# Five attention blocks of a decoder: the turned maxima are added to the queries in PSUM instead of on VectorE

## What is computed

```
Q = (x @ wq.T + bq).reshape(B, S, 16, 8)      K, V likewise (K, V from ctx in the cross blocks)
score  = einsum('bhqd,bhkd->bhqk', Q, K) / sqrt(8)
attn_w = softmax(score, axis=-1)
out    = einsum('bhqk,bhkd->bhqd', attn_w, V) ... @ wo.T + bo
x      = layernorm(x + out)
```

## Time and profile before

| | us |
|---|---|
| median of 3 runs | 423.5 |
| lowest and highest of them | 422.8, 425.97 |
| the profiled execution, its own time | 421.75 |
| its span, first to last instruction | 419.9 |
| busy: PE | 374.2 (89%) |
| busy: weight loads of PE | 330.0 (79%) |
| busy: VectorE | 283.9 (68%) |
| busy: ScalarE | 224.8 (54%) |

### The profile page before, as it was taken

One profiled execution on the slowest core, in us unless ns is written; L12 is line 12 of the kernel. 1 busy time (PEld: TensorE's weight loads), 2 busy tenths in 40 slices (PEclk: granted clock), 3 DMA queues, 4 the chain that ended last, 5 costly groups with the idle time before them and its releaser, 6 DMA issues.

```text
span 419.9 us, 9114 instructions
## 1 busy us (share of the span) xinstructions
PE 374.2 (89%) x3274; PEld 330.0 (79%) x3274; DVE 283.9 (68%) x840; ACT 224.8 (54%) x526; POOL 54.5 (13%) x62
## 2 busy tenths in 40 slices
PE   4578899999889999699998999999997999889991
PEld 3467777787779898689987898978996878768891
DVE  6598889888965556722678346563469898873773
ACT  2145566665665564566436664676552767562331
POOL 7700004910000000000000000000003000101124
PEclk9699999999999999699998999999999999999996
DMA  5646311214340000200011000011003021472031
GB/s 157 196 144 215 114 45 33 73 33 119 110 135 18 2 2 0 77 2 0 2 39 37 2 2 2 0 39 40 2 4 86 2 77 32 149 236 64 12 113 34
DMA packets 23644, 25.68 MB, mean 61 GB/s; under 512 B 3241, under 2 KB 18354, under 8 KB 23601
## 3 DMA queue, kind: packets, MB, share of 16 engines
q1 hardware_dynamic: 22128, 23.47, 18.9%
q0 software_dynamic: 512, 0.97, 0.7%
q10 hardware_dynamic: 960, 0.66, 0.6%
HBM read 18.35 MB, written 6.83 MB: 60 GB/s over the span
## 4 chain that ended last, share of the span: by engine, by line
PE 71%; DVE 18%; issue 5%; ACT 2%; DMA 2%; POOLq 0%; SPq 0%; POOL 0%; ACTq 0%; DVEq 0%
PE bank_D L851 13%; PE bank_C L737 10%; PE bank_D L709 9%; PE bank_A L720 8%; DVE negmax L1250 5%; PE bank_A L867 4%; PE bank_A L869 4%; PE bank_A L868 4%; PE bank_D L635 2%; PE bank_D L768 2%; PE bank_D L693 2%; PE bank_A L655 1%; PE bank_D L751 1%; PE bank_D L1585 1%; PE bank_D L645 1%
## 5 line engine op out<-in xcount | busy, mean ns | idle before, releaser
L1250 DVE TENSOR_REDUCE negmax<-bank_D 128x2 f32<-128x512 f32 x192 | 127.7, 685 | 40.2 <-PE bank_D L709 39.5
L997 ACT ACTIVATE expo<-bank_A 128x512 f32<-128x512 f32 x192 | 109.7, 596 | 49.0 <-PE bank_A L720 47.3
L709 PE MATMUL bank_D<-k_head,q_sp 128*128 128x256 f32 x384 | 89.0, 317 | 7.3 <-DVE negmax L1250 3.5
L720 PE MATMUL bank_A<-q_sp,k_head 128*128 128x256 f32 x384 | 81.6, 297 | 4.1 <-DVE q_sp L1245 3.9
L1033 ACT ACTIVATE hidden<-bank_A,b 128x256 f32<-128x256 f32 x128 | 53.7, 471 | 54.8 <-PE bank_A L869 54.8
L709 PEld LDWEIGHTS bank_D<-k_head,q_sp 128*128 128x128 f32 x384 | 60.2, 196 | 19.5 <-issue 8.9
L851 PE MATMUL bank_D<-mix_w,hidden 128*128 128x128 f32 x512 | 67.9, 276 | 0.9 <-DVE qk_lo L1125 0.9
L720 PEld LDWEIGHTS bank_A<-q_sp,k_head 128*128 128x128 f32 x384 | 59.9, 192 | 6.7 <-DVE q_sp L1245 5.5
L851 PEld LDWEIGHTS bank_D<-mix_w,hidden 128*128 128x128 f32 x512 | 62.6, 192 | 2.2 <-issue 2.1
L737 PE MATMUL bank_C<-expo,v_aug 128*32 128x256 f32 x768 | 46.4, 382 | 0.6 <-ACT expo L997 0.3
L1309 DVE SCALAR_TENSOR_TENSOR y_mixture<-bank_D,g_w,y_mixture 128x128 f32<-128x128 f32 x64 | 22.3, 348 | 30.3 <-PE bank_D L851 26.2
(11 more groups left out here) (195 smaller groups left out, 515.8 us busy)
## 6 DMA issues: line engine op xcount, KB each, us to landing
mix_w<-in_mix_w SPq DMA_DIRECT2D x24, 256.0 KB, 3.5
k_head<-k_scratch SPq DMA_DIRECT2D x92, 48.0 KB
k_scratch<-qk_hi SPq DMA_DIRECT2D x24, 128.0 KB, 2.4
w_last<-in_mix_w SPq DMA_DIRECT2D x8, 256.0 KB, 6.1
k_scratch<-qk_lo SPq DMA_DIRECT2D x12, 128.0 KB, 2.3
proj_w<-in_proj SPq DMA_DIRECT2D x1, 640.0 KB, 5.2
xe_scratch<-empty_row SPq DMA_DIRECT2D x1, 520.0 KB, 4.2
expo<-xe_scratch SPq DMA_DIRECT2D x2, 260.0 KB, 3.2
```

Of the source, the lines that this page charges most:

```text
L709: last = mm(where(seq, b, ("max", k))[:, qt * SEQ:(qt + 1) * SEQ], q_sps[SET[seq, b]][:, k // 4, qt * P:(qt + 1) * P], k_heads[SET[seq, b] ...
L720: last = mm(where(seq, b, ("exp", h))[:, kt * SEQ:(kt + 1) * SEQ], k_heads[SET[seq, b]][:, t, g, kt * P:(kt + 1) * P], q_sps[SET[seq, b]][ ...
L997: activate(expo[:, exp_slot(seq, b, h), :], where(seq, b, ("exp", h))[:], ACT.Exp, scale=float(HD) ** -0.5).then_inc(free(seq, b, ("exp", ...
L1250: V.tensor_reduce(negmaxes[SET[seq, b]][:, s // 4, :, 32 * (s % 4)], where(seq, b, ("max", s))[:].rearrange("p (q n) -> p q n", q=QT), AX. ...
```

## The change

For the first five blocks (`LAID_TWICE = 5`), the shift is done another way. After the two transposes PE lays the queries out once more on top of them, in the same bank: the two matmuls of the spread for this group (high and low part, 256 columns each) with accumulation. ScalarE then copies the sum into `q_sp`, after its exponential of the same step. VectorE's addition goes. The bank is now freed by ScalarE's copy, which PE's score by key of the group also waits for. The queries' parts must live longer for that, so `qk_hi` and `qk_lo` get a third part, and blocks alternate between parts 0 and 2 for their queries. The other seven attention blocks are as before.

```diff
+LAID_TWICE = 5
+def laid_twice(seq, b):
+    return ORDER[seq, b] < LAID_TWICE
+def q_part(seq, b):
+    return 2 * SET[seq, b]
...
-        qk_hi = sb("qk_hi", [P, 2, SEQ], f32r)
-        qk_lo = sb("qk_lo", [P, 2, SEQ], f32r)
+        qk_hi = sb("qk_hi", [P, 1 + SETS, SEQ], f32r)
+        qk_lo = sb("qk_lo", [P, 1 + SETS, SEQ], f32r)
...
@@ TensorE, shift
-                    for qt in range(QT):
-                        last = nc.tensor.transpose(
-                            where(seq, b, ("shift", t))[:, qt * P:(qt + 1) * P],
-                            negmaxes[SET[seq, b]][:, t, qt, :], ident)
+                    dst = where(seq, b, ("shift", t))[:, 0:SEQ]
+                    if laid_twice(seq, b):
+                        for qt in range(QT):
+                            mm(dst[:, qt * P:(qt + 1) * P], negmaxes[SET[seq, b]][:, t, qt, :], ident,
+                               start=(qt == 0), stop=False, is_transpose=True)
+                        mm(dst, spread[:, QHI, t, :], qk_hi[:, q_part(seq, b), :],
+                           start=False, stop=False)
+                        last = mm(dst, spread[:, QLO, t, :], qk_lo[:, q_part(seq, b), :],
+                                  start=False, stop=True)
+                    else:
+                        for qt in range(QT):
+                            last = nc.tensor.transpose(dst[:, qt * P:(qt + 1) * P],
+                                                       negmaxes[SET[seq, b]][:, t, qt, :], ident)
...
@@ ScalarE, after the exponential of the step
+                        t = group_at(s, SHIFT_AT)
+                        if t is not None and laid_twice(seq, b):
+                            wait_filled(act, seq, b, ("shift", t))
+                            activate(q_sps[SET[seq, b]][:, t, :],
+                                     where(seq, b, ("shift", t))[:, 0:SEQ], ACT.Copy
+                                     ).then_inc(free(seq, b, ("shift", t)), 1)
...
@@ VectorE
-                        if group_at(s, SHIFT_AT) is not None:
+                        if group_at(s, SHIFT_AT) is not None and not laid_twice(seq, b):
```

More of the change, by code:

```diff
@@ L654, in spread_rows @@
                             dst = where(seq, b, f"sq{half}")[:, (t % 2) * SEQ:(t % 2 + 1) * SEQ]
-                            mm(dst, spread[:, QHI, t, :], qk_hi[:, 0, :], start=True, stop=False)
-                            last = mm(dst, spread[:, QLO, t, :], qk_lo[:, 0, :], start=False, stop=True)
+                            mm(dst, spread[:, QHI, t, :], qk_hi[:, q_part(seq, b), :],
+                               start=True, stop=False)
+                            last = mm(dst, spread[:, QLO, t, :], qk_lo[:, q_part(seq, b), :],
+                                      start=False, stop=True)
                         last.then_inc(full(seq, b, f"sq{half}"), 1)
@@ L945, in high @@
                     wait_filled(act, seq, b, what)
-                    activate(qk_hi[:, i, :], where(seq, b, what)[:, 0:SEQ],
+                    activate(qk_hi[:, i if i else q_part(seq, b), :], where(seq, b, what)[:, 0:SEQ],
                              ACT.Identity, bias=bias).then_inc(high_ready[seq], 1)
@@ L1124, in low @@
                     dve.wait_ge(high_ready[seq], 2 * (MHA[b] - 1) + 2 - i)
-                    V.scalar_tensor_tensor(qk_lo[:, i, :], where(seq, b, what)[:, 0:SEQ], bias,
-                                           qk_hi[:, i, :].bitcast(f32), ALU.add, ALU.subtract
+                    part = i if i else q_part(seq, b)
+                    V.scalar_tensor_tensor(qk_lo[:, part, :], where(seq, b, what)[:, 0:SEQ], bias,
+                                           qk_hi[:, part, :].bitcast(f32), ALU.add, ALU.subtract
                                            ).then_inc(free(seq, b, what), 1)
@@ L1142, in split @@
                     link(V.tensor_tensor(rope[:, 0, :], rope[:, 0, :], rope[:, 1, :], ALU.add))
-                    rounded = V.tensor_copy(qk_hi[:, i, :], rope[:, 0, :])
+                    part = i if i else q_part(seq, b)
+                    rounded = V.tensor_copy(qk_hi[:, part, :], rope[:, 0, :])
                     if what == "k":
@@ L1148, in split @@
                         link(rounded)
-                    V.tensor_tensor(qk_lo[:, i, :], rope[:, 0, :], qk_hi[:, i, :].bitcast(f32),
+                    V.tensor_tensor(qk_lo[:, part, :], rope[:, 0, :], qk_hi[:, part, :].bitcast(f32),
                                     ALU.subtract).then_inc(ready[seq], 1)
```

## The result

| | before | changed |
|---|---|---|
| median of 18 runs each | 422.8 us (421.5 to 427.5) | 427.2 us (424.5 to 430.0) |
| span of the profiled execution | 419.9 us | 425.4 us |
| ratio of the times | | 1.0105, 95% interval 1.0087 to 1.0123 |

The changed kernel is about 1% slower, some 4.4 us (the interval is 3.7 to 5.2). The prediction was +2.3 us, with 419.5 to 429.7 as its range. The time lies inside the range, on the side that was forecast, and between the forecast and rival 1 (+5.6). The extra time is about twice what was summed.

A forecast was written before the change was run, and what follows sets the result against it. PE and VectorE were taken to hand the bound to each other several times per block. Terms 0.81 - 0.28 + 0.91 + 0.89 - 0.05 + 0 gave +2.3 us on a 423.5 median: 425.8 us, range 419.5 to 429.7.

The forecast's parts named there:

- rival 1: All five blocks: PE's added 0.24 counts at every shift, plus the third groups' new waits; +5.6 us, 429.1; chance 0.17.
- third group, first block: Step 14, first block: PE, not held up before, now waits for ScalarE's copy, so the values start later; +0.91 us.
- third group, second, fourth and fifth: Step 14: PE's wait for VectorE's addition becomes a wait for ScalarE's copy; +0.27 us each, +0.81 together.
- third group, third block: Step 14, third block: VectorE is the bound, so its removed 0.32 counts, less 0.04 for a root; -0.28 us.
- fourth groups, with the first ones behind them: Step 18: PE's 0.24 counts in three blocks, 0.17 in the first, together +0.89; step 6: 0 to -0.05 us.
- second groups: Step 10: +0.12 us each in the second and fifth block, -0.12 each in the third and fourth; together 0.
- Rival 2: VectorE is the bound, so each removed addition gives 0.32 back; at most -6.4 us, 417.1, half 420.3; chance 0.22.
- Rival 3: Third groups: ScalarE's copy is ready before PE asks, so the old wait really goes; 422.4 us; chance 0.13.

The follow-up runs named there:

- e4: Changed kernel, but the third group of each of the five blocks has VectorE's addition back; 424.7 us against 423.2 before, ratio 1.0031.
- e3: Changed kernel with only the third group of each of the five blocks laid twice, the others as before; 426.8 us against 423.2, ratio 1.0064.
- e1: Changed kernel with ScalarE's copy put ahead of the exponential of the same step; 426.0 us against 423.2 before, ratio 1.0068.
- e5: Changed kernel without its 40 added matmuls, transposes and ScalarE's copies kept; 424.8 us against 423.1 before, ratio 1.0039.
- e11: Changed kernel, all 20 shifts, with ScalarE's copy ahead of the exponential and its root behind head 7's exponential; 425.5 us against 422.9 before, ratio 1.0045.
- e2: Changed kernel with VectorE making the copy at its old addition's place, instead of ScalarE; 425.8 us against 423.2 before, ratio 1.0065.
- e8: Kernel before, with only the second to fifth blocks' third groups changed, copy ahead of the exponential, root one tick later; 422.25 us against 423.09, ratio 0.9973.

## Why the prediction was right, and where its sizes were off

Term by term, from the distances between value stretches in the timelines. The third groups are the change less e4, where they are as before; the third block's is e3's:

| term | predicted | measured |
|---|---|---|
| third group, first block | +0.91 | +0.83 |
| third group, second, fourth and fifth | +0.81 | +1.08 (0.36, 0.36, 0.36) |
| third group, third block | -0.28 | -0.04 |
| fourth groups, with the first ones behind them | +0.84 | +1.21 (0.22, 0.28, 0.25, 0.21, 0.25) |
| second groups | 0 | +0.41 (0.22, -0.02, -0.01, 0.22) |
| first block, a gap before the rotation | not seen | +0.40 |
| sum | +2.3 | +3.9 |

The block length says +3.94 and +4.02. The sum closes to 0.1.

**Is it right by luck?** The mechanism and the sign are as told. The size is not: the measured 4.4 is nearly twice the 2.3, and at 1.05% (0.87 to 1.23) it lies on the edge of the 1% within which the prediction put a chance of 0.68. The median of 427.2 falls inside the forecast's own 424.5 to 427.5 partly because the 423.5 it was added to was 0.7 too high (422.8 with 18 runs).

**The third groups** went as told for head 8's score: the copy's place behind the exponential put it 0.28 later in the second block and exactly where forecast in the first. The values are where the sizes went wrong. The prediction let them follow that score by 0.98, which is the chain's figure for the second block. In the timeline it is 0.91 there (51.85 to 52.76), and 0.90 in the first block of the changed kernel (32.58 to 33.48), so +0.91 was 0.08 too much. In the later blocks a second bound stands close behind, head 7's exponential behind the root. I had found it to end at 53.0 against 53.10 for the values and called it nothing. It holds the values 0.09 longer in the second block of the changed kernel, where they start 0.13 behind its end; 0.27 became 0.36. A margin of 0.1 is no cover. In e3's profile the second block has +0.63, of which 0.26 is time between the root and that exponential for which no releaser is recorded.

**The third block.** I called VectorE the bound and gave its removed 0.32 back. It came back as nothing. Timeline of the kernel before, and of the changed one, at this place:

```profile
70.09 1.29 POOL L505 TENSOR_TENSOR w_lo<-mix_w,w_hi 128x512 fp32r<-128x512 f32 x1
70.91 0.48 DVE L1177 SCALAR_TENSOR_TENSOR newton_attention<-mv_attention,const,r_attention 128x2 f32<-128x2 f32 x1
```

```profile
71.30 0.69 POOL L506 TENSOR_TENSOR xb<-x_rows,rows 128x256 f32<-128x256 f32 x1 [17.93 <-DVE y_attention L1260]
...
72.63 1.28 POOL L516 TENSOR_TENSOR w_lo<-mix_w,w_hi 128x512 fp32r<-128x512 f32 x1
...
73.11 0.81 DVE L1207 SCALAR_TENSOR_TENSOR newton_attention<-mv_attention,const,r_attention 128x2 f32<-128x2 f32 x1
```

VectorE's small operation starts earlier in its turn, but lasts 0.81 instead of 0.48. It ends at 73.92, with GpSimd's `w_lo` (72.63 + 1.28 = 73.91). Before it was the same: 70.91 + 0.48 = 71.39, and 70.09 + 1.29 = 71.38. GpSimd's two split operations follow its own `xb`, which is released by the older block's sum, not by the addition. From the start of `xb` to the end of this operation the trace has 2.62 in the kernels before and after, 2.63 in e3 and 2.64 in e4, with or without the addition. So neither VectorE's work nor its queue was the bound for that operation. It points to something that it shares with GpSimd. The Trainium skill has such a thing (SBUF — State Buffer, Who interferes with whom): VectorE and GpSimd share a port pair under an exclusive lock. The trace agrees in the ends. That it is this port was not tried.

**The fourth groups.** PE's full 0.24 was right for the second, fourth and fifth block (0.28, 0.21, 0.25), and holds for the first too (0.22, where I had 0.17). I let the third block's be absorbed, because PE waits for VectorE near it. That wait, for the turn of the rows, stands ahead of the group's transposes and not behind them. Chain of the changed kernel:

```profile
74.70 1.76 DVE x_rows L1212 x2
76.47 0.14 issue
76.60 0.41 PE bank_A L801 x2
77.01 0.27 PE bank_D L708 x2
77.28 0.12 PE bank_D L710
```

Nothing behind 77.01 waits for several heads, so the group costs 0.25 as the others do. A wait absorbs only what comes before it.

**The second groups.** In the second and fifth block I had taken half of PE's 0.24 as absorbed, since VectorE's rotation began 0.15 behind PE's projection. Timeline of the changed kernel there:

```profile
47.12 0.59 PE L648 MATMUL bank_D<-xT_all,proj_w 128*128 128x256 f32 x2
...
47.82 0.48 DVE L1162 SCALAR_TENSOR_TENSOR rope<-bank_D,cols,const 128x256 f32<-128x256 f32 x1 [0.46 <-PE bank_D L648]
```

VectorE has been idle for 0.46 and still starts 0.11 behind the projection's end: nearly all of the 0.15 was the usual distance, not slack. From the first block's second value stretch, the projection moved by 0.24 and the rotation by 0.20. In the third and fourth block the restart was indeed skipped, but that paid for PE's 0.24 and no more. In the third block's chain the pair behind the earlier trace rows had held 0.51 before, and it holds 0.24 in the changed kernel (68.88):

```profile
66.07 0.51 PE bank_D L709 x2
```

**The gap before the first block's rotation.** In both profiles of the change, and in e1, e5 and e11, VectorE starts the first rotation some 0.4 later behind PE's projection; in e2, e3 and e4 it does not, nor where no queries are laid twice. So it was seen only where ScalarE copies all 20 shifts. Chain of the changed kernel, then of e4:

```profile
37.22 0.45 PE bank_D L648 x2
37.67 0.03 issue
37.70 0.02 DVEq L450
37.72 0.46 issue
38.18 0.48 DVE rope L1162
```

```profile
36.64 0.02 DVEq L450
36.66 0.04 issue
36.71 0.48 DVE rope L1162
```

The stretch of 0.46 is "issue": no releaser is recorded. The addition is gone from this place in e4 too. It repeats in five profiles, so it is no accident; its cause stays open.

**The rivals.** Rival 1 had the sign and part of the mechanism: of the shifts outside the third groups that the measure covers, seven cost 0.21 to 0.28 each and the others about nothing, 1.6 together where it had 3.6. The first groups are among the free ones, as the earlier trace rows said. Rival 2, VectorE as the bound, falls with VectorE's idle time for PE's scores, which grew from 7.7 to 15.8 while no value stretch came earlier, and with e5. What the relief would be worth with PE's matmuls gone and ScalarE's two orders mended was not run. Rival 3 falls with PE's five waits for the copy. e1 and e8 show that its price was wrong too: with the copy back in time a third group gave 0.32 at most, where it had 0.64.

## What to carry to other kernels

Where two engines hand the bound to each other, price a moved operation at each place, and ask at each place for the second-latest input of what waits, and for the third: here head 7's exponential stood 0.05 to 0.1 us behind a wait of 0.45, and behind that stood the moments, the root and the turn of the rows. Take both starts of a distance from one view: a chain that cuts overlaps and a timeline that keeps them differ by 0.07 us per start. A small operation moved to an engine with room costs its place in that engine's queue, not its duration; put it ahead of the long operation whose result is needed later. A wait absorbs added work only if it stands behind that work, and the 0.1 us that lay here between a producer and its consumer everywhere is no slack.

## What the runs showed of the hardware

- Two fp32 transposes and then two accumulating fp32r matmuls of 256 columns go into one bank as one group and cost 0.22 + 0.12 + 0.12 on PE at the full clock. At the half level the same took 0.43 + 0.21 + 0.21 (the changed kernel at 23.95 us).
- A VectorE operation on 128x2 elements took 0.21 in the second block and 0.81 in the third, where GpSimd was at work, and it ended within 0.01 us of GpSimd's operation.
- A copy of 256 columns from PSUM costs 0.378 on ScalarE and 0.414 on VectorE, where the addition of PSUM to SBUF had cost 0.41: for VectorE a copy is no cheaper than the addition.
- With the distances inside the five blocks repeating to 0.06 us, single executions of one kernel still differ by up to 6.0 us (421.5 to 427.5 before, 424.5 to 430.0 changed). The profiles show the granted clock at its lower level at different times, such as 0.77 at 24 to 28 us in one and 1.00 in another.
